# W2 rebuilt by four products on VectorE, biases added ahead into the destination slot, statistics kept per chunk, and every engine's order laid out anew

## What is computed

```python
x = x + 0.5 * ffn(layernorm(x), W1, b1, W2, b2, scale)
x = x + attn(layernorm(x), Wq, bq, Wk, bk, Wv, bv, Wo, bo, R)
x = x + 0.5 * ffn(layernorm(x), W1, b1, W2, b2, scale)
# ffn: lt are tokens 1 to 16 of each sequence
even, odd = lt[:, ::2, :], lt[:, 1::2, :]
m1 = (even[:, :4, :, None] * odd[:, :4, None, :]).reshape(B, 512, 128)
m2 = (even[:, 4:, :, None] * odd[:, 4:, None, :]).reshape(B, 128, 512)
h = gelu(x @ W1.T + scale * (x @ m1.T) + b1)
out = h @ W2.T + scale * (h @ m2.T) + b2
# attn: 16 heads of 8; q', k' = exp(q R - |q|^2 / 2)
out = (q' (k'^T v)) / (sum(q') + 1e-8) @ Wo.T + bo
```

## Time and profile before

| | |
|---|---|
| runs | 191.19, 191.21 and 191.68 us, median 191.21 |
| profiled execution | span 190.5 us, from its first to its last instruction |
| PE busy | 172.3 us (90%), 1115 matmul records |
| DVE busy | 152.1 us (80%), 485 instructions |
| ACT busy | 96.8 us (51%) |
| POOL busy | 96.7 us (51%), 124 instructions |
| chain that ended last | PE 55%, DVE 19%, issue 11%, DMA 7%, POOL 3% |

### The profile page before, as it was taken

One profiled execution on the slowest core, in us unless ns is written; L12 is line 12 of the kernel. 1 busy time (PEld: TensorE's weight loads), 2 busy tenths in 40 slices (PEclk: granted clock), 3 DMA queues, 4 the chain that ended last, 5 costly groups with the idle time before them and its releaser, 6 DMA issues.

```text
span 190.5 us, 3499 instructions
## 1 busy us (share of the span) xinstructions
PE 172.3 (90%) x1115; PEld 150.9 (79%) x1115; DVE 152.1 (80%) x485; ACT 96.8 (51%) x170; POOL 96.7 (51%) x124
## 2 busy tenths in 40 slices
PE   6859979997989999999999988789989979988994
PEld 6746968896978899877888877469969968876993
DVE  2794999999999737699999999987796897688111
ACT  3126514582666599697845475544434607425420
POOL 4707752781796651259754542945475371573000
PEclk9988999999999999999999999969999999999999
DMA  6849300030030000000000003001202311140303
GB/s 139 222 135 252 109 6 0 3 109 3 5 110 5 0 0 0 3 2 0 0 3 0 0 2 112 0 3 44 69 0 58 112 57 55 34 137 23 87 3 110
DMA packets 17921, 9.60 MB, mean 50 GB/s; under 512 B 880, under 2 KB 17520, under 8 KB 17904
## 3 DMA queue, kind: packets, MB, share of 16 engines
q1 hardware_dynamic: 17904, 9.38, 17.5%
HBM read 7.22 MB, written 2.16 MB: 49 GB/s over the span
## 4 chain that ended last, share of the span: by engine, by line
PE 55%; DVE 19%; issue 11%; DMA 7%; POOL 3%; ACT 2%; SPq 0%; DVEq 0%; POOLq 0%; ACTq 0%
PE quad L732 21%; PE quad L718 6%; DVE xn L546 6%; PE quad L720 5%; PE quad L719 5%; DMA ev<-token_rows 3%; PE ps_t L690 3%; PE quad L749 3%; DMA rows<-in_rows_dram 3%; PE quad L751 3%; PE quad L750 3%; DMA token_rows<-xn 1%; PE ps_g L767 1%; DVE ex L630 1%; DVE bst L177 1%
## 5 line engine op out<-in xcount | busy, mean ns | idle before, releaser
L478 ACT ACTIVATE gl<-quad,cols 128x512 f32<-128x512 f32 x64 | 43.5, 687 | 47.2 <-PE quad L720 46.4
L732 PEld LDWEIGHTS quad<-w2e,gl 128*128 128x128 f32 x496 | 60.8, 192 | 2.5
L732 PE MATMUL quad<-w2e,gl 128*128 128x128 f32 x496 | 62.0, 275 | 0.0
L546 DVE TENSOR_SCALAR xn<-X,mv,rstd 128x128 f32<-128x128 f32 x64 | 31.5, 555 | 6.2 <-POOL rstd L198 6.2
L718 PE MATMUL quad<-xh,w1h 128*128 128x512 f32 x64 | 29.4, 460 | 5.2 <-issue 4.0
L719 PE MATMUL quad<-xl,w1h 128*128 128x512 f32 x64 | 26.4, 413 | 0.0
L720 PE MATMUL quad<-xh,w1l 128*128 128x512 f32 x64 | 26.2, 410 | 0.0
L415 POOL TENSOR_TENSOR X<-X,b2h 128x512 f32<-128x512 f32 x16 | 20.4, 1281 | 8.7 <-DVE xn L546 8.7
L196 POOL TENSOR_SCALAR veps<-mv 128x4 f32<-128x4 f32 x16 | 4.3, 270 | 33.9 <-DVE mv L189 33.9
L614 DVE TENSOR_TENSOR X<-quad,X 128x512 f32<-128x512 f32 (+1 forms) x16 | 10.5, 658 | 13.6 <-PE quad L732 13.6
L718 PEld LDWEIGHTS quad<-xh,w1h 128*128 128x128 f32 x64 | 12.5, 196 | 8.9 <-issue 7.7
(11 more groups left out here) (91 smaller groups left out, 305.2 us busy)
## 6 DMA issues: line engine op xcount, KB each, us to landing
ev<-token_rows SPq DMA_DIRECT2D x8, 512.0 KB, 3.8
X<-in_x_dram SPq DMA_DIRECT2D x8, 256.0 KB, 5.3
out_dram<-X SPq DMA_DIRECT2D x7, 256.0 KB, 2.3
w1t<-in_w1t_dram SPq DMA_DIRECT2D x1, 256.0 KB, 5.4
w2n<-in_w2t_dram SPq DMA_DIRECT2D x1, 256.0 KB, 5.2
wa<-in_wa_dram SPq DMA_DIRECT2D x1, 256.0 KB, 5.8
out_dram<-X SPq DMA_DIRECT2D x2, 128.0 KB, 1.8
rows<-in_rows_dram SPq DMA_DIRECT2D x1, 128.5 KB, 5.3
```

The source lines that it names most:

```text
L478: act.activation(gl[:, f % 2, j], ps_h[j % 2], ACT.Gelu, bias=cols[:, j:j + 1]).then_inc(s_gelu, 1)
L546: dve.tensor_scalar(xn[:, i % 2, n], X[:, xslot(i), n], mv[:, i % 2, n, 0:1], rstd[:, i % 2, n:n + 1], ALU.subtract, ALU.mult).then_inc(s_ ...
L732: ins = pe.matmul(y[:, n * P:(n + 1) * P], gl[:, f % 2, j, n * P:(n + 1) * P], w2e[:, f // PER_B % 2, j], start=(j == 0), stop=(j == HB - 1))
```

## The change

- W2 leaves POOL: in stage `w2` DVE makes it by four scalar_tensor_tensor products of 128 elements each, even token times `od` plus `w2t`, straight into `w2e`. For sequence 0 they read the bank `ps_r`, into which PE spreads the even tokens by four more products (new stage `select`), so transfer `rows.0` is gone.
- The adds of half b2 and of bo write into the slot of X that the block's result goes to, and no longer wait for the norm: `bias` waits for the load (or for `s_x2`), `abias` for `s_x1`.
- `stats`, `moments`, `veps` and `rstd` have a buffer for each chunk; `veps` is made on DVE (24 times). `xn`, `xh` and `xl` are three chunks deep, `qt` three instead of four; `ev` has two buffers and `od` one per build.
- From sequence 1 on, `w1h` and `w1l` are made in one instruction of 512 each after all four `w1r`; for sequence 0 block by block.
- Chunk 0 is loaded in three pieces on SP and ACT's queue, `scale`, W2 and the columns on ACT's queue too; `b2h` is a stage of its own.
- The orders are written out as lists. The norm of a token stays on DVE.

```diff
-TIMES = {
+ORDER = {
...
     "pool": (
-        {
-            "stats": (-0.68, -1.2), "norm": (-0.65, 0.33), "w2": (1.31, None),
-        },
+        "stats.0 stats.1 stats.2 stats.3 stats.4 bias.0 bias.1 bias.2 stats.5 stats.6 astats.0 bias.3 stats.7 "
+        "astats.1 bias.4 bias.5 astats.2 astats.3 astats.4 bias.6 bias.7 astats.5 abias.0 abias.1 abias.2 abias.3 "
+        "abias.4 astats.6 abias.5 abias.6 astats.7 z.0 z.1 z.2 z.3 abias.7 z.4 stats.8 z.5 bias.8 bias.9 stats.9 "
+        "stats.10 z.6 stats.11 stats.12 z.7 stats.13 stats.14 bias.10 bias.11 bias.12 bias.13 bias.14 stats.15 "
+        "bias.15 "
...
-def moments(dve, i, bst, mv, s_bst, s_mv, s_rstd, s_xn):
-
+def moments(dve, i, bst, mv, veps, s_bst, s_mv, s_veps):
 
     dve.wait_ge(s_bst, i + 1)
-    if i >= 2:
-        dve.wait_ge(s_rstd, i - 1)
-        dve.wait_ge(s_xn, NT * (i - 1))
     for n in range(NT):
-        ins = dve.bn_aggr(mv[:, i % 2, n], bst[:, i % 2, n])
+        ins = dve.bn_aggr(mv[:, i, n], bst[:, i, n])
     ins.then_inc(s_mv, 1)
-
+    dve.wait_ge(s_mv, i + 1)
+    dve.tensor_scalar(veps[:, i], mv[:, i, :, 1], LN_EPS, None, ALU.add).then_inc(s_veps, 1)
...
-                    sp.dma_start(token_rows[i], xn[1:1 + 4 * LORA, 0, 0, :]).then_inc(s_rows, 16)
-                    sp.wait_ge(s_rows, 16 * (i + 1))
-
-                    wait(sp, s_w1r, LORA * i)
-                    wait(sp, s_w2m, i)
+                    sp.dma_start(token_rows[i], xn[1:1 + 4 * LORA, PER_B * i % XN, 0, :]).then_inc(s_rows, 16)
+                    sp.wait_ge(s_rows, 16 * i)
+
+
+                    wait(sp, s_w1r, LORA * (i - 1))
+                    wait(sp, s_w2, LORA * (i - 1))
                     even = token_rows[i].rearrange("(n two) d -> two n d", two=2)[0]
-                    sp.dma_start(ev[:], even.partition_broadcast(P)).then_inc(s_ev, 16)
+                    sp.dma_start(ev[:, i % 2], even.partition_broadcast(P)).then_inc(s_ev, 16)
...
-                if stage == "norm":
-
-                    pool.wait_ge(s_xn, NT * (i + 1))
-                    if i == 0:
-                        pool.wait_ge(k_b2h, 1)
-                    pool.tensor_tensor(X[:, xslot(i)], X[:, xslot(i)], b2h[:].unsqueeze(1).to_broadcast([P, NT, D]),
+                    pool.tensor_scalar(anmr[:, i], amr[:, i], -1.0, SHIFT, ALU.mult, ALU.add).then_inc(a_nmr, 1)
...
+                    before, after = (i, CHUNKS + i) if i < CHUNKS else (i + CHUNKS, i - CHUNKS)
+                    pool.tensor_tensor(X[:, after], X[:, before], b2h[:].unsqueeze(1).to_broadcast([P, NT, D]),
                                        ALU.add).then_inc(s_xb, 1)
-                if stage == "anorm":
-                    pool.wait_ge(a_xn, NT * (i + 1))
-                    pool.tensor_tensor(X[:, CHUNKS + i], X[:, CHUNKS + i],
+                if stage == "abias":
+
+                    pool.wait_ge(s_x1, i + 1)
+                    pool.tensor_tensor(X[:, 2 * CHUNKS + i], X[:, CHUNKS + i],
                                        rows[:, D:2 * D].unsqueeze(1).to_broadcast([P, NT, D]), ALU.add).then_inc(a_xb, 1)
-                if stage == "w2":
-                    pool.wait_ge(s_ev, 16 * (i + 1))
-                    pool.wait_ge(s_od, i + 1)
-                    wait(pool, s_w2, i)
-                    pool.tensor_tensor(w2m[:], ev[:, LORA:2 * LORA],
-                                       od[:, LORA:2 * LORA].unsqueeze(2).to_broadcast([P, LORA, D]),
-                                       ALU.mult).then_inc(s_w2m, 1)
-                    pool.wait_ge(s_w2m, i + 1)
-                    if i == 0:
-                        pool.wait_ge(k_w2t, 1)
-
-                    wait(pool, s_d, NT * PER_B * (i - 1))
-                    pool.tensor_tensor(w2e[:, i % 2], flat(w2m[:]).rearrange("p (o k) -> p k o", k=HB),
-                                       w2t[:], ALU.add).then_inc(s_w2, 1)
...
-                        dve.wait_ge(s_ev, 16 * (i + 1))
+                        dve.wait_ge(s_ev, 16 * i)
...
-                    even = ps_m[:].rearrange("p (j d) -> p j d", j=LORA) if i == 0 else ev
-
-                    for j in range(LORA + 2):
-                        if j < LORA:
-                            dve.scalar_tensor_tensor(out=w1r[:, j], in0=even[:, j], scalar=od[:, j:j + 1],
+                    even = ps_m[:].rearrange("p (j d) -> p j d", j=LORA) if i == 0 else ev[:, i % 2]
+
+
+                    blocks = LORA if i == 0 else 1
+                    for k in range(blocks):
+                        mine = range(LORA * k // blocks, LORA * (k + 1) // blocks)
+                        part = slice(D * mine[0], D * (mine[-1] + 1))
+                        for j in mine:
+                            dve.scalar_tensor_tensor(out=w1r[:, j], in0=even[:, j], scalar=od[:, i, j:j + 1],
                                                      in1=w1t[:, j * D:(j + 1) * D], op0=ALU.mult,
                                                      op1=ALU.add).then_inc(s_w1r, 1)
-                        if 1 <= j <= LORA:
-                            dve.wait_ge(s_w1r, LORA * i + j)
-                            if j == 1:
-
-                                wait(dve, s_u, HB * PER_B * (i - 1))
-                            dve.tensor_copy(w1h[:, i % 2, (j - 1) * D:j * D], w1r[:, j - 1]).then_inc(s_w1h, 1)
-                        if j >= 2:
-                            blk = slice((j - 2) * D, (j - 1) * D)
-                            dve.wait_ge(s_w1h, LORA * i + j - 1)
-                            dve.tensor_tensor(w1l[:, i % 2, blk], w1r[:, j - 2], w1h[:, i % 2, blk].bitcast(F32),
-                                              ALU.subtract).then_inc(s_w1, 1)
+                        dve.wait_ge(s_w1r, LORA * i + mine[-1] + 1)
+                        wait(dve, s_u, HB * PER_B * (i - 1))
+                        dve.tensor_copy(w1h[:, i % 2, part], flat(w1r[:])[:, part]).then_inc(s_w1h, LORA // blocks)
+                        dve.wait_ge(s_w1h, LORA * i + mine[-1] + 1)
+                        dve.tensor_tensor(w1l[:, i % 2, part], flat(w1r[:])[:, part],
+                                          w1h[:, i % 2, part].bitcast(F32), ALU.subtract).then_inc(s_w1, LORA // blocks)
+                if stage == "w2":
+                    dve.wait_ge(s_od, i + 1)
+                    if i == 0:
+                        dve.wait_ge(k_w2t, 1)
+                        dve.wait_ge(k_sel2, 1)
+                    else:
+                        dve.wait_ge(s_ev, 16 * i)
+                    even = ps_r[:].rearrange("p (j d) -> p j d", j=LORA) if i == 0 else ev[:, i % 2, LORA:]
+
+                    wait(dve, s_d, NT * PER_B * (i - 1))
+                    for j in range(LORA):
+                        out_rows = slice(j * D // LORA, (j + 1) * D // LORA)
+                        dve.scalar_tensor_tensor(out=w2e[:, i % 2, :, out_rows],
+                                                 in0=even[:, j].rearrange("p (o k) -> p k o", k=HB),
+                                                 scalar=od[:, i, LORA + j:LORA + j + 1], in1=w2t[:, :, out_rows],
+                                                 op0=ALU.mult, op1=ALU.add).then_inc(s_w2, 1)
```

More of the change, by code:

```diff
@@ L75 @@
     ),
     "dve": (
[L77 to L87, removed]
@@ L160, in plan @@
-def plan(engine):
-    placed = []
-    for stage, i, phase, step in work():
-        name = f"{stage} {i[1]}" if isinstance(i, tuple) else stage
-        time = TIMES[engine][phase].get(name, (None, None))[step % 2]
-        if time is not None:
-            placed.append((step + APART.get((engine, stage, i), time), stage, i))
-    placed.sort(key=lambda p: p[0])
-    return [(stage, i) for _, stage, i in placed]
-def stats(dve, i, x, bst, s_bst, s_mv):
-    if i >= 2:
-        dve.wait_ge(s_mv, i - 1)
[17 rows of a table added]
+    ),
+}
@@ L244, in build @@
         w1l = sb("w1l", [P, 2, H], F32R)
-        w2m = sb("w2m", [P, LORA, D])
         w2e = sb("w2e", [P, 2, HB, D])
         cols = sb("cols", [P, HB + 3])
-        rows = sb("rows", [P, 2 * D + 1])
+        rows = sb("rows", [P, 2 * D])
+        scale = sb("scale", [P, 1])
         b2h = sb("b2h", [P, D])
@@ L351, in _ @@
             sp.dma_start(rrep[:], r_in.partition_broadcast(HEADS)).then_inc(ld_r, 16)
+            for c in range(3, CHUNKS):
+                sp.dma_start(X[:, c], chunk_of(x, c)).then_inc(ld_x[c], 16)
             for stage, i in plan("sp"):
@@ L532, in _ @@
                 if stage == "stats":
-                    if i < CHUNKS:
+                    if i == 0:
+                        for n in range(3):
+                            dve.wait_ge(ld_x0[n], 16)
+                    elif i < CHUNKS:
                         dve.wait_ge(ld_x[i], 16)
@@ L548, in _ @@
                 if stage == "scale":
+                    dve.wait_ge(ld_scale, 16)
+                    s = scale[:].to_broadcast([P, LORA])
+                    dve.tensor_copy(scl[:, 0:LORA], s).then_inc(k_scl, 1)
```

(4 more changed lines are left out.)

256 lines of the change are left out of this document (90 added, 166 removed), and 45 rows, old and new, of the table ORDER.

## The result

The changed kernel takes **182.24 us** (median of 4 runs, 182.09 to 182.55) against 191.20 before (4 runs beside it, 191.18 to 191.68): a ratio of 0.9552, 95% interval 0.9514 to 0.9589. The profiled execution took 182.55 us with a span of 180.8, against 190.5. Where executions show a slower state too, the numbers here leave it out. The forecast was 181.6, with a span of 180.9. As will be seen, the sum came out nearly right in part by luck: its errors cancelled.

What follows compares the result with a forecast made beforehand. PE's stream was taken to set the time, its waits almost always for DVE, overfull or held by POOL. Gains of 10.9 less new waits of 1.3 gave -9.6: span 180.9, plus 0.7 around it, 181.6 us; range 176.0 to 187.5.

Steps and rivals of the forecast that it cites:

- W2's hold on PE: PE waits caused by POOL's W2 rebuilds locking out DVE: 7.6 us in all, of which 6.5 were taken as gain.
- The products: W2's 32 new products on DVE, 0.26 us each as for `w1r`: 8.4 us, at most 16.8.
- DVE's account: Change in DVE's time: -14.5 stalls, +8.4 products, +5.0 epsilons, -2.0 merged casts and subtractions, together -3.1 us.
- The bias adds' holds: DVE stalls beside POOL's other long instructions stay at 10.3 us; five adds in a row near the end cost 0.5.
- The start: First norm no longer waits for `b2h`; first up product at 12.05 instead of 12.56 us, a gain of 0.5.
- `xal` at 56 us: PE's wait behind a late `xal`, whose norm two adds had locked: 0.7 of 0.9 us gained.
- The join at 113 to 122: Waits for `X`, `w1l` and `qn`, where the new order puts other products between: 1.0 of 1.7 us gained.
- The clock: Half-clock stretch at 125.29 to 128.69 us, after PE stood still: 1.2 of 1.7 us gained.
- New waits: Losses of 1.3 us: 0.5 five adds, 0.4 up products waiting for a whole W1 rebuild, 0.4 anything else then last.
- DVE as the bound: Rival: DVE's load, not its stalls, bounds the kernel, so only 5.9 us are gained: 185.3 us, chance 0.20.
- The lock turned round: Rival: DVE's products delay POOL's powers by 0.6 us each, half on the path, 7.2 back: 188.8 us, chance 0.07.
- More collisions: Rival: POOL's long adds meet two-operand DVE work more often than the present 12 of 32: slower, 196.5 us, chance 0.05.

## Why the prediction came out nearly right

*W2's hold on PE (7.6, taken 6.5)*: right in mechanism, and a little too low. None of the eight waits counted is in the new trace. Running W2 on POOL in the new order costs 3.8 us from the statistics on and in the old one 6.9 more than products on DVE, clock included. But the prediction gave these waits to the move alone, and the new arrangement with W2 left on POOL wins 7.3 us too. One stall of the 14.5 us, 0.76 at 120.89, also stands beside `qn` and not beside W2.

*The products (8.4 us)*: mis-sized. 28 take 0.35 us from start to start, the four from PSUM 0.26: 28 x 0.35 + 4 x 0.26 = 10.8 us, 2.4 more. The rule named in the prediction (the Trainium skill, "SBUF — State Buffer", section "Door 1: The DMA port swizzle") was right against my choice: `ev` is strided by 16 bytes in SBUF and pays a third, not double; straight reads pay nothing. But those 2.4 us did not reach the end, as the run with straight reads shows.

*DVE's account (-3.1)*: measured -1.9. The products cost 2.4 more than put down and the epsilons 1.4 more (6.4 for 5.0); the merged casts and subtractions gave back more than 2.0, from 17.9 us to 9.9, ends of holds included.

*The bias adds' holds (10.3 left, 0.5 for five in a row)*: the number was right, the place was not. In the new trace eight `xn`, one `veps`, one `aveps` and one product are held, about 9.9 us. The five in a row cost PE 0.38 up to 153.11, against 0.5. What I did not see are three in a row at 28.29, behind a `b2h` that now comes late, for which PE waits 1.30 us up to 33.30. Moving the adds gives 1.5 us.

*The start (+0.5)*: wrong in sign. The first up product came at 14.07 where 12.05 was forecast: this step failed by 2.0 us. It assumed that chunk 0 lands in time for statistics at 3.69; with loads on the second queue they began at 5.15, 1.46 later. The other 0.56 is the path from the first norm to that product, forecast at 5.65 us and measured at 6.21 (7.86 to 14.07), with 0.27 of DVE waiting for `xh` in it. The "no row shows" in it concerned only the scale; the change put four loads on ACT's queue, and that should have been a term.

*`xal` at 56 us (0.7)*: gone, right. *The join at 113 to 122 (1.0)*: wrong; the three waits went, and 0.64 for `kvm`, 0.85 for `qk` and 0.26 before an up product came, 1.75 in place of 1.7: nothing gained.

*The clock (1.2)*: the stretch at 125.29 is gone as a whole, 1.7 us. The other, at 12.65, was no term at all: it slowed the first twelve up products, which took 4.76 us (12.56 to 17.32) and now take 3.69 (14.07 to 17.76), since the stretch falls on fillers. Neither belongs to the kernel before as such: in its runs beside the experiments the mean granted clock goes from 0.973 to 1.0, and 1.0 is no such stretch, so how much of the gain is the clock's depends on the execution.

*New waits (1.3)*: those for whole rebuilds of W1 hardly show (0.3); the `xl` up to 33.30 (1.30) and a `gl` up to 35.84 (0.48) do.

Sum against sum, from the first up product to the end, first of the kernel before, then of the changed one (length, then PE's busy time):

```profile
12.56:190.50 177.94, 163.99 (x1069) 143.56 (x1069) 144.32 (x450) 94.03 (x166) 90.74 (x107) 0.98 0.15 43
```

```profile
14.07:180.83 166.76, 158.90 (x1070) 140.29 (x1069) 142.89 (x462) 93.98 (x167) 63.94 (x70) 1.00 0.12 36
```

The first up product comes 1.5 us later, PE's idle time behind it falls by 6.1 (13.95 to 7.86) and its busy time by 5.1: 9.7, where 9.6 were forecast. The forecast had +0.5 for the start, 6.9 for waits less new ones, and 2.2 for clock and refill. So 2.0 were lost at the start and 0.8 at the waits, and 2.9 more than forecast came from PE's busy time: 1.2 of it in the first twelve up products, 0.5 at 125 us, and the rest in refills, which no run parts from other causes. That these meet at 0.1 us is luck; the mechanism, PE waiting for DVE instructions that POOL holds, is not.

*Rivals.* DVE as the bound (185.3) is near what the old order gives, 184.75, where 32 products cost 6.8 us. The new order escapes it, which I had given as its "against" without a number. The lock turned round (188.8) did not occur: the power has a mean of 1023 ns, less than the 1090 before. More collisions (196.5) did not occur: 9.9 us, not 31.

## What to carry to other kernels

Take a two-input elementwise instruction off the engine that holds another one up, even where the other is the fuller of the two, and lay the order out anew: here the move alone gave 6.9 us, the new arrangement alone 7.3, both 11.1. So test the order without the move as well, before the gain is put down to either. Look at which long instructions of POOL stand beside which of DVE, one by one; moving nine adds by a few microseconds, with the same work, gave 1.5 us. Count every load that a change moves to another queue as a term of its own, and read its landing against the load on which the first instruction waits. Look for stretches at half clock in the trace that the forecast starts from: what work they fall on is a term too.
